# First context tiles with loads and places of their own, one at every second tile pair, and V's last outputs awaited in the attention

## What is computed

```python
x = x + L0_xattn(layernorm(x), ctx, lens)     # depooling scan
x = x + L0_attn(layernorm(x))                 # mamba block
x = x + L0_ffn(layernorm(x))                  # ternary feed-forward
x = x + L1_xattn(layernorm(x), ctx, ...)      # cross attention: this case
x = x + L1_attn(layernorm(x))                 # head attention
x = x + L1_ffn(layernorm(x))                  # experts
```

```python
q = split_heads(x @ Wq) * scale
k, v = split(context @ Wkv)                   # context: 8 x 1601 x 1024
sim = q @ [null_k, k].T
out = softmax(sim) @ [null_v, v]
out = layernorm(out @ Wout)
```

## Time and profile before

| | |
|---|---|
| three runs | 3136.47, 3142.53, 3144.61 us; median 3142.53 |
| the profiled execution | 3140.0 us, span 3138.3 us |
| PE, matmul | 2843.9 us busy, 91% of the span |
| DVE, ACT, POOL | 52%, 34% and 8% of the span |
| DMA queue of SP | 40.0% of 16 engines' span |
| the 17 pairs | from 1014.8 to 1350 us |
| the attention | from 1357 to 2613 us |

### The profile page before, as it was taken

The page is one execution under the profiler, slowest core; times in us unless marked ns, Lnnn a source line. Parts: engine busy times, 40 slices in busy tenths (PEclk is TensorE's granted clock), DMA queues, the critical chain, the costliest instruction groups (busy, mean ns, idle before and its releaser), DMA issues. The chain is left out here.

```text
span 3138.3 us, 42368 instructions
## 1 busy us (share of the span) xinstructions
PE 2843.9 (91%) x17657; PEld 1531.3 (49%) x17657; DVE 1635.9 (52%) x1937; ACT 1063.4 (34%) x1643; POOL 245.0 (8%) x325
## 2 busy tenths in 40 slices
PE   6999999988989998989999999999999995827899
PEld 3334444433444443446565666666666662515453
DVE  5359999994645655633434343434343433286310
ACT  3254444332524333422323232333332320483210
POOL 1000000000001644600000000000000000010000
PEclk9999999999999999999999999999999997857899
DMA  5133243333324433445555565555564542120203
GB/s 200 37 120 88 89 145 98 94 114 128 124 82 160 128 101 107 129 120 119 141 119 140 119 147 118 151 119 147 120 147 113 113 92 63 53 60 7 108 10 137
DMA packets 473781, 345.84 MB, mean 110 GB/s; under 512 B 232340, under 2 KB 437461, under 8 KB 468984
## 3 DMA queue, kind: packets, MB, share of 16 engines
q1 hardware_dynamic: 473592, 343.15, 40.0%
HBM read 230.79 MB, written 54.62 MB: 91 GB/s over the span
## 5 line engine op out<-in xcount | busy, mean ns | idle before, releaser
L1829 PE MATMUL ca_p_s<-early_halves,ca_qw 128*128 128x448 f16 (+2 forms) x1408 | 467.2, 332 | 1.4 <-DVE ca_qw L1952 1.4
L1830 PE MATMUL ca_p_s<-early_halves,ca_qw 128*128 128x448 f16 (+2 forms) x1408 | 467.3, 332 | 0.0
L1831 PE MATMUL ca_p_s<-early_halves,ca_qw 128*128 128x448 f16 (+2 forms) x1408 | 467.1, 332 | 0.0
L1952 DVE TENSOR_TENSOR ca_qw<-ca_p_w,ca_qw 128x512 f16<-128x512 f32 x128 | 88.5, 691 | 508.2 <-ACT ca_qw L1899 508.2
L393 PE MATMUL vw_pv<-vw_wv,vw_ctx 128*128 128x512 f16 (+1 forms) x688 | 263.7, 383 | 37.4 <-PEq L74 15.3
L394 PE MATMUL vw_pv<-vw_wv,vw_ctx 128*128 128x512 f16 (+1 forms) x688 | 263.6, 383 | 0.0
L395 PE MATMUL vw_pv<-vw_wv,vw_ctx 128*128 128x512 f16 (+1 forms) x688 | 263.1, 382 | 0.0
L1899 ACT ACTIVATE ca_qw<-ca_p_w 128x512 f16<-128x512 f32 x128 | 76.4, 597 | 506.4 <-PE ca_p_w L1810 506.4
L1830 PE MATMUL ca_p_s<-ca_ctx,ca_qw 128*128 128x448 f16 (+2 forms) x640 | 216.2, 338 | 0.0
L1829 PE MATMUL ca_p_s<-ca_ctx,ca_qw 128*128 128x448 f16 (+2 forms) x640 | 216.2, 338 | 0.0
L1831 PE MATMUL ca_p_s<-ca_ctx,ca_qw 128*128 128x448 f16 (+2 forms) x640 | 216.1, 338 | 0.0
(11 more groups left out here) (555 smaller groups left out, 5409.0 us busy)
## 6 DMA issues: line engine op xcount, KB each, us to landing
ca_stage<-in_ctx_t SPq DMA_DIRECT2D x97, 512.0 KB, 3.5
vd<-vw_vst SPq DMA_DIRECT2D x192, 256.0 KB, 2.3
ca_vals<-vd SPq DMA_DIRECT2D x64, 768.0 KB
vw_ring<-in_ctx_t SPq DMA_DIRECT2D x94, 512.0 KB, 4.0
ex_w_d<-in_w_d SPq DMA_DIRECT2D x8, 2048.0 KB, 8.0
vw_ring<-in_w_kv SPq DMA_DIRECT2D x16, 512.0 KB, 4.6
early_r<-state_rows SPq DMA_DIRECT2D x8, 1024.0 KB, 8.2
early_r<-in_w SPq DMA_DIRECT2D x2, 4096.0 KB, 12.6
```

Of the source, the lines that this page charges most:

```text
L1829: nc.tensor.matmul(o, a[:, 0, c, :], x[:, 0, c, lo:hi], start=(c == 0), stop=False)
L1830: nc.tensor.matmul(o, a[:, 0, c, :], x[:, 1, c, lo:hi], start=False, stop=False)
L1831: last = nc.tensor.matmul(o, a[:, 1, c, :], x[:, 0, c, lo:hi], start=False, stop=(c == CC - 1))
L1952: nc.vector.tensor_tensor(qw[f % 2][:, 1, c, :], p_w[:, :].rearrange("p (c n) -> p c n", n=P), qw[f % 2][:, 0, c, :], ALU.subtract).then_i ...
```

## The change

The seven first tiles leave the list `loads`, so that tiles alone go through the ring. Each first tile is loaded by two DMAs of its own (one for each half of a tile's 128 columns), which move pieces of 64 f32. It goes to the place of first tile 5 or 6 in the output buffer (`FIRST_PLACE`), as raw f32, and the seventh goes to ring slot 2 when pair 15 has used it. Steps 3, 5, ..., 15 have the two instructions that split one of them (`FIRST_AT`). SP issues the loads one step ahead, between the tile loads and the stores of its step. The semaphores of V's stores are held by the stage `early`, the waits for them leave the end of `cq`, and `attend` has them in SP's program behind its first three tile loads (`drain`).

```diff
     def __init__(... )   # ValueWork
+        self.quad_out = [outer.sem(f"quad_out{s}") for s in range(4)]
...
-    FIRST_FROM = 4
+    FIRST_AT = {3 + 2 * n: n for n in range(FIRST_TILES)}
+    FIRST_PLACE = [6, 5, 6, 5, 6, 6]
...
-        self.v_out = [st.sem(f"q_out{s}") for s in range(4)]
+        self.ld_first = st.sem("ld_first")
+        whole = region[:, 0:28 * 512].bitcast(f32).rearrange("p (l c n) -> p c l n", l=2, c=CC)
+        self.first_raw = [whole[:, :, :, n * (P // 2):(n + 1) * (P // 2)] for n in self.FIRST_PLACE]
+        self.first_raw.append(self.raws[2 * vw.QUADS % self.RAWS].rearrange("p (c l n) -> p c l n", l=2, c=CC))
+        self.v_out = vw.quad_out
         for i in range(vw.QUADS):
             self.loads += [("tile", 2 * i), ("tile", 2 * i + 1)]
-            if 0 <= i - self.FIRST_FROM < self.FIRST_TILES:
-                self.loads.append(("first", i - self.FIRST_FROM))
...
+    def load_first(self, sp, n):
+        if n == self.FIRST_TILES - 1:
+            sp.wait_ge(self.op_lo, 3 * (self.vw.QUADS - 1))
+            sp.wait_ge(self.s_made, 4 * (self.vw.QUADS - 1))
+        else:
+            before = [m for m in range(n) if self.FIRST_PLACE[m] == self.FIRST_PLACE[n]]
+            if before:
+                sp.wait_ge(self.f_lo, before[-1] + 1)
+        source = self.vw.io.ctx_t[0, n, :, :].rearrange("p (c l n) -> p c l n", l=2, c=CC)
+        for l in range(2):
+            sp.dma_start(self.first_raw[n][:, :, l, :], source[:, :, l, :]).then_inc(self.ld_first, 16)
...
     def sp(self, sp):
...
+            if i + 1 in self.FIRST_AT:
+                self.load_first(sp, self.FIRST_AT[i + 1])
             for k, (t, g) in enumerate(self.OUTS):
...
-            if ("first", i + 2 - self.FIRST_FROM) in self.index:
-                self.load(sp, self.index["first", i + 2 - self.FIRST_FROM])
+
+    def drain(self, sp):
         for k in range(4):
-            vw.all_out(sp, k)
-            sp.wait_ge(self.v_out[k], self.outs_before(vw.QUADS, k))
+            sp.wait_ge(self.v_out[k], self.outs_before(self.vw.QUADS, k))
...
     def first_high(self, act, n):
+        act.wait_ge(self.ld_first, 32 * (n + 1))
+        if n:
+            act.wait_ge(self.f_lo, n)
+        self.nc.scalar.activation(self.first_place(n, 0), self.first_raw[n], ACT.Copy).then_inc(self.f_hi, 1)
...
     # attend, SP
             for i in range(-HERE, 3 - HERE):
                 load(i)
+            quads.drain(sp)
             load_values(0)
             load_values(1)
```

More of the change, by code:

```diff
@@ L252, with __init__ @@
     UNITS = 2 * WHOLE
-    def __init__(self, nc, io, st, vd, wkt, first_half, before_queries):
+    def __init__(self, nc, io, st, outer, vd, wkt, first_half, before_queries):
         self.nc, self.io, self.vd, self.wkt, self.first_half = nc, io, vd, wkt, first_half
@@ L548, in load @@
         else:
[L549 to L557, removed]
+            sp.wait_ge(self.op_lo, 3 * ((k - self.RAWS) // 2 + 1))
+            sp.wait_ge(self.s_made, 4 * ((k - self.RAWS) // 2 + 1))
+        sp.dma_start(self.raws[k % self.RAWS], vw.tile_source(vw.WHOLE + k)).then_inc(self.ld[k % self.RAWS], 16)
+    def load_first(self, sp, n):
[9 more added lines that the diff above has]
+            sp.dma_start(self.first_raw[n][:, :, l, :], source[:, :, l, :]).then_inc(self.ld_first, 16)
     def loaded(self, engine, load):
@@ L683, in first_place @@
     def first_place(self, n, l):
-        return self.vw.first_half[0][:, l, :, n * P:(n + 1) * P]
+        return self.vw.first_half[0][:, l, :, n * P:(n + 1) * P].rearrange("p c (l n) -> p c l n", l=2)
     def first_high(self, act, n):
-        raw = self.loaded(act, ("first", n))
-        self.nc.scalar.activation(self.first_place(n, 0), raw.rearrange("p (c n) -> p c n", n=P), ACT.Copy)\
-            .then_inc(self.f_hi, 1)
+        act.wait_ge(self.ld_first, 32 * (n + 1))
+        if n:
+            act.wait_ge(self.f_lo, n)
+        self.nc.scalar.activation(self.first_place(n, 0), self.first_raw[n], ACT.Copy).then_inc(self.f_hi, 1)
     def first_low(self, dve, n):
-        raw = self.loaded(dve, ("first", n))
         dve.wait_ge(self.f_hi, n + 1)
-        self.nc.vector.tensor_tensor(self.first_place(n, 1), raw.rearrange("p (c n) -> p c n", n=P),
-                                     self.first_place(n, 0), ALU.subtract).then_inc(self.f_lo, 1)
+        self.nc.vector.tensor_tensor(self.first_place(n, 1), self.first_raw[n], self.first_place(n, 0),
+                                     ALU.subtract).then_inc(self.f_lo, 1)
     def begin_act(self, act):
@@ L756, in act @@
             self.out_high(act, i, 3)
-            if ("first", i - self.FIRST_FROM) in self.index:
-                self.first_high(act, i - self.FIRST_FROM)
+            if i in self.FIRST_AT:
+                self.first_high(act, self.FIRST_AT[i])
     def dve(self, dve):
@@ L779, in dve @@
             self.out_low(dve, i, 3)
-            if ("first", i - self.FIRST_FROM) in self.index:
-                self.first_low(dve, i - self.FIRST_FROM)
+            if i in self.FIRST_AT:
+                self.first_low(dve, self.FIRST_AT[i])
 COLS = dict(g_res=(0, 4), conv_b=(4, 8), d_skip=(12, 8), dt_b=(20, 8), conv_w=(28, 32))
@@ L1664, in _, with attend @@
             quads.dve(dve)
-def attend(nc, io, k, q_parts, o_t, vd, wkt, halves):
+def attend(nc, io, k, q_parts, o_t, vd, wkt, halves, quads):
     with Stage(nc, "ca") as st:
@@ L3167, in build @@
             with Stage(nc, "vw") as st:
-                vw = ValueWork(nc, io, st, io.vd, wkt, halves, 123)
+                vw = ValueWork(nc, io, st, early, io.vd, wkt, halves, 123)
                 depool_stream(nc, io, k, vw, x, xn, xt, region)
@@ L3172, in build @@
                 queries(nc, io, k, vw, x, xn, xt, q_parts, region)
-            attend(nc, io, k, q_parts, o_t, io.vd, wkt, halves)
+            attend(nc, io, k, q_parts, o_t, io.vd, wkt, halves, vw.quads)
         project_out(nc, io, k, x, o_t)
```

## The result

| | before | changed |
|---|---|---|
| median | 3139.69 us (4 runs) | 3110.72 us (4 runs) |
| range | 3136.47 to 3144.61 | 3104.64 to 3114.06 |
| ratio | | 0.9904, 95% interval 0.9880 to 0.9928 |
| profiled execution | 3140.0, span 3138.3 | 3107.78, span 3105.7 |

The change makes the kernel 0.96% faster, 29.0 us by the medians. The forecast was 27.9 us less, 3114.6 us. Of the 3.9 us between that time and the measured one, 2.8 come from the kernel before itself, whose median is 3139.7 us over four runs and was 3142.5 over the three shown ahead of the forecast.

What follows compares the result with a forecast made beforehand. It took PE as the bound, busy 91% of the span, with 26.9 us lost in the pairs. -26.9 - 1.6 + 0.6 = -27.9 us against the median of 3142.5 gave 3114.6 us, range 3107 to 3126.

Steps and rivals of the forecast that it cites:

- The loss on PE: In the 17 tile pairs: PE's gaps, from tile loads waiting for slots that first tiles hold, vanish; gain 26.9 us.
- not the ring: Rival, in the pairs: late loads are a symptom, something else holds the operands, only the ends count; 3141.5 us, chance 0.04.
- The splits: At every second pair: at worst 2.3 us each on ACT and DVE, covered by PE's pace; taken as 0, upper bound 16.
- the step of 15.0 us: In the pairs: the time ACT, DVE and POOL need per pair without late loads, 3.1 us below PE's 18.13.
- Half of it: Rival, in the pairs: splits are not covered, PE pays 2.3 us for each of seven, 16 us; 3130.6 us, chance 0.09.
- The slow clock: In the pairs: matmuls behind PE's gaps run at 1.2 GHz, about 5 us of the 26.9 lost.
- The small loads: First tiles as two DMAs of 256-byte pieces: about 7 us, issued some 18 us ahead of use; taken as 0.
- small pieces hold the queue: Rival, in the DMA queue: next tile loads stand behind small pieces, costing PE from about 37 us a tile; slower, chance 0.03.
- SP's new waits: In SP's program: waits for earlier low parts are two steps old or delay two stores some 5 us; taken as 0.
- The ends: Stage end and behind the attention: moved drain saves 1.6 us, an added barrier costs 0.6.

Runs made afterwards that it cites:

- splits in a row: The changed kernel with the first six first tiles split at consecutive steps 4 to 9, the seventh still at step 15: 3113.27 us, ratio 0.9917 to the kernel before.
- ring, spaced: The kernel before with its first tiles still in the ring, but at pairs 3, 5, ..., 15: 3125.31 us, ratio 0.9958 to the kernel before.

## Why the prediction was right

**The loss on PE and its cause.** 26.9 us were forecast for PE, and the pairs became 26.91 us shorter. That the ring held back the tile loads is shown: with first tiles out of the ring the waits vanish, however the splits are placed (splits in a row), and with first tiles left in it they stay, however they are placed (ring, spaced). The rival "not the ring" is out by the same two kernels. One thing moved together with the place, and no run separates it: SP now issues a first tile's load ahead of the stores of its step, where it stood behind them. For the slot speaks the trace of the kernel before: in each of the seven steps SP issues the held tile load 0.03 us after DVE has ended the split (1111.03 and 1111.06 in the first, 1252.26 and 1252.28 in the last).

**The splits.** Taken at 0, and 0 they are. Doubling them cost nothing and four of them cost 13 us with the stage's end, so the cover is there and so is the step of 15.0 us that it was reckoned from. "Half of it" is out.

**The slow clock.** The 5 us of matmuls at 1.2 GHz behind the gaps went with the gaps: the granted clock is 1.00 through the pairs now.

**The small loads.** 0 was right. The row it stood on (512 KB in eight DMAs in about 7 us) was close for two larger DMAs: from the first issue to the last landing they take 6.3 to 7.4 us where they stand right behind two tile loads. The Trainium skill, DMA: Bandwidth & Descriptors, section Specifications, wants at least 512 bytes for full rate. In kind the trace agrees, but the price is small: the seventh first tile, which has no tile load right before it, has landed 4.5 us after its first issue, against 4.0 for 512 KB in 4 KB rows (on the page of the profile before). By the DMA packets in the trace the 16 engines spend 2.6 us on a first tile and 1.5 on a tile of 4 KB rows. None of it reaches PE. The step that failed is one in the rival "small pieces hold the queue": it priced the transfer, put the decision at 37 us and named the tile loads. The runs showed SP's issue as what grows, about 20 us as the point, and the stores, which ACT awaits, as what comes late. The changed kernel holds SP for 1.3 us, so the forecast didn't hang on it.

**SP's new waits.** One reading was wrong and cost nothing. The last load into place 6 (first tile 5, counted from 0) waits for a split that is not two steps old: DVE ended it at 1238.20 and SP issued the load at 1238.23.

**The ends.** Expected -1.6 and +0.6, measured -1.82 (5.50 for 7.32) and +0.39 (1.64 for 1.25). SP's wait of 1.6 us was nearly all of the first. The other was sized from the two barriers of the earlier trace rows, 0.6 us apart; why the new one is 0.2 us shorter isn't shown.

**The rest.** The medians differ by 29.0 us where the change's three lines give 28.3; the profiled executions by 32.2, with 4.3 of it outside anything that was changed. That share lies within the spread of the same stretches over the experiments.

## What to carry to other kernels

A load that shares a ring with others makes the loads behind it wait for its consumer. Where that consumer stands at the end of a step, give the load a place of its own, if only in an output buffer that is not yet final, rather than a gentler rhythm. To price such a change, take the span of the engine that sets the pace, less its count of instructions times the time from one start to the next where it has no gap; and take the rate of the others from a stretch in which they catch up. Then ask what stands behind the new DMAs in the issuing engine's program: stores that someone awaits count as much as loads.

## What the runs showed of the hardware

- Cutting the same 512 KB into more DMAs costs SP more than the DMA engines here. From 2 DMAs (2048 pieces) to 16 (16384 pieces) the DMA share of the 308 us rose by 15.3 points (41.5% to 56.8%), which is 6.7 us of all 16 engines for each of the seven tiles, while SP's issue went from 1.3 to 15.3 us for each. Every such DMA had 1024 pieces, so these runs don't tell the cost of a DMA to SP from that of its pieces; a tile load of 128 rows of 4 KB takes SP 0.4 us, against 0.67.
- SP reaches the barrier with stores still in flight: in the changed kernel its last store is issued at 1325.32 and lands at 1327.80, and the attention begins at 1327.60.
- Stages without any change differ between executions: the last part by up to 7.2 us (520.0 to 527.2), more than all that the ends of this change are worth (1.4 us).
